# Moving layer-norm statistics of a Mamba and mixture-of-experts layer from GpSimd to ScalarE and VectorE

## The chip, the cores and the metric

The kernel runs on one core of a Trainium2 chip. The metric is device time in microseconds (us), the median of several runs of the whole kernel. A core has five engines with a queue of their own each: TensorE (PE in the profile, its weight loads PEld), VectorE (DVE), ScalarE (ACT), GpSimd (POOL) and SyncE (SP, which issues DMAs). Each engine runs its own instructions in the order in which they were written, and engines wait for one another through semaphores.

## The reference

One layer of a sequence model over x of 32 sequences, 512 tokens, 256 features, all in float32. Cut to what matters here:

```python
def _layernorm(x, axis=-1, eps=1e-05):
    m = jnp.mean(x, axis=axis, keepdims=True)
    v = jnp.var(x, axis=axis, keepdims=True)
    return (x - m) / jnp.sqrt(v + eps)

def _L0_attn_ref(x, ln_g, ln_b, ...):
    skip = x
    xn = (x - mu) * jax.lax.rsqrt(var + 1e-05) * ln_g + ln_b
    xp, z = split(xn @ in_proj_w.T)                  # 512 channels each
    xc = silu(causal depthwise conv of 4 taps (xp) + conv_b)
    dt, Bm, Cm = split(xc @ x_proj_w.T)              # 16, 16, 16
    dt = softplus(dt @ dt_proj_w.T + dt_proj_b)
    A = -jnp.exp(A_log)
    # h_t = exp(dt_t * A) * h_{t-1} + dt_t * xc_t * Bm_t ; y_t = sum_n h_t * Cm_t
    y = _selective_scan(xc, dt, A, Bm, Cm, D) * silu(z)
    g = gelu(y @ out_proj_w.T) @ glu_w.T + glu_b
    return g[..., :256] * sigmoid(g[..., 256:]) + skip

def _L0_ffn_ref(x, ...):
    shared = (silu(gu[:, :512]) * gu[:, 512:] @ shared_down_w) * sigmoid(x @ shared_gate_w)
    probs = softmax(x @ gate_w)                      # 64 experts, the best 8 of each token
    # each expert takes its first 128 tokens: silu(gate) * up, then down, weighted
    return y + shared

x = x + _L0_attn_ref(_layernorm(x), ...)
x = x + _L0_ffn_ref(_layernorm(x), ...)
```

So the first block normalizes twice in a row (once outside, once inside with its own eps). From the variance v of x one needs (v + eps)^(-1/2) and, for the two norms as one, (v (1 + eps) + eps^2)^(-1/2).

## The kernel before

The 32 sequences run one after the other. A sequence of 512 tokens takes 32 steps s: two halves of the 512 channels times 16 states n. A step works on one tile of 128 partitions x 1024 (two channel blocks of 512 tokens). In each step:

- ACT writes the two decays exp(dt * A) into PSUM (`decays`, L537), two steps ahead;
- POOL multiplies dt*x by B into a ring of eight tiles (`scan_input`, L377), three steps ahead;
- DVE runs the scan along the tokens (L1165) and multiplies the state by C (L1175); for the 15 steps of the table `ON_POOL`, POOL makes that product instead (`read_state`, L386);
- PE adds the transposed product to a sum in PSUM (`sum_states`, L814).

The first product of half 0 (`y` times silu(z)) is taken by DVE at step 18, that of half 1 at step 2 of the next sequence (`gate_y`, L1078), once PE has summed all 16 states.

Around this skeleton every engine carries, inside the same 32 steps, the work that comes after the scan of the sequence before ("post": out projection, gelu, gated unit, second norm, router, shared expert) and the work ahead of the scan of the next one ("prep": norm, input projection, conv, silu, dt). What is done at which step is written by hand in a table of numbers at the end of the file (`SOFT_AT`, `SCALES2`, `NORM2` and so on); each engine walks through it in order of s, and within a step in the order of its own function `turn`. The first two and last two sequences are written out, the 28 between are a hardware loop of 14 rounds with two sequences each, so every second change of sequence is also the loop's jump. Behind the 32 sequences stands the stage of the 64 experts (gathers, small matmuls, scatters).

The places that matter here:

- `moments` (L1051, L1055): mean and variance of x by DVE, for the first norm at step 20 (`MOMENTS0`, two sequences ahead), for the second at step 15 (`MOMENTS2`).
- `scales_x` (L390 to L407, POOL, step 29) forms from them the two reciprocal roots with `pow`, the shifts -mean * root, and 1 + root, six small instructions; `scales_x1` (L409 to L419, POOL, step 15) the same for the second norm, four instructions.
- ACT uses them in `norm_x` (L545, step 1), `sum_x` (L552, step 17) and `norm_x1` (L560, step 15).
- `step_sizes` (L428) and `step_inputs` (L433, L435) on POOL: a DMA that adds two parts of dt in memory, then dt times x, then a mark at the first token. The mark (`dt_ready`) releases the decays of the next sequence on ACT and its scan inputs on POOL. For half 0 they stand at steps 28 and 29, for half 1 at 8 and 9. In POOL's queue `scales_x` stands ahead of `step_inputs` of step 29.
- softplus on ACT: `soft_exp` (L614) and `soft_log` (L619), the logarithm at steps 27 and 6.
- After silu_z (L597, step 29) ACT's next work is the decays of the next sequence; at step 0 `read_dt` (L608, L609) copies the two last dt blocks of half 1, between which PE has to run `project_dt` (L858) and after which PE sums the last state (L814).

ACT holds one set of function tables at a time; the program loads a set (ACT_TABLE_LOAD) ahead of an activation whose function is not in the one that is held.

Of the kernel before, what the change touches and what calls it, by code (L numbers as in the profile page):

```python
# [9 lines left out]
ALU = mybir.AluOpType  # L10
# [30 lines left out]
def mamba_moe(nc, x, vectors, in_wT, conv_w, x_wT, dt_wT, a_log, out_wT, glu_wT, router_w, sgu_w, sdown_w, egu_w, edown_w, out, counts, table, ends, bc):  # L41
    ctx = ExitStack()
    with ctx:
# [43 lines left out]
        minus_half = sb("minus_half", [P, 2 * NT])  # L87
# [58 lines left out]
        scales0_ready, scales2_ready = sem("scales0_ready"), sem("scales2_ready")  # L146
        prep_full, prep_read = sem("prep_full"), sem("prep_read")
# [204 lines left out]
        def _(pool):  # L352
# [4 lines left out]
            pool.memset(minus_half[:, :], -0.5).then_inc(cleared, 1)  # L357
# [32 lines left out]
            def scales_x(k):  # L390
                wait_apart(pool, ln0, 3 * k + 2)
                pool.tensor_scalar(rstd[:, 0, :].unsqueeze(2), mv[:, 0, :, 1:2], EPS, None, ALU.add)\
                    .then_inc(scales0_ready, 1)
                pool.tensor_scalar(rstd[:, 1, :].unsqueeze(2), mv[:, 0, :, 1:2], 1.0 + EPS, EPS * EPS,
                                   ALU.mult, ALU.add).then_inc(scales0_ready, 1)
                pool.tensor_scalar(keep[:, :].unsqueeze(2), mv[:, 0, :, 0:1], -1.0, None, ALU.mult)\
                    .then_inc(scales0_ready, 1)
                pool.wait_ge(scales0_ready, 6 * k + 2)
                pool.tensor_tensor(rstd[:, 0:2, :], rstd[:, 0:2, :],  # L399
                                   minus_half[:, :].rearrange("p (a i) -> p a i", a=2), ALU.pow)\  # L400
                    .then_inc(scales0_ready, 1)
# [35 lines left out]
            def turn(b, h, prep, post):  # L437
                p, q = b + 1, b - 1
                for s in range(NS):
# [4 lines left out]
                    if post and s == SCALES2:  # L444
                        scales_x1(q)
# [75 lines left out]
        def _(act):  # L521
# [199 lines left out]
            def post_at(q, h, s):  # L721
# [11 lines left out]
                if s == G_AT[1] + AFTER_G:  # L733
                    glu_gate(q)
# [636 lines left out]
```

## Time and profile before

| | us |
|---|---|
| median of 3 runs | 4621.09 |
| lowest and highest | 4621.03, 4624.51 |
| profiled execution, from its first to its last instruction (span) | 4617.3 |
| median less that span (start and end of the run around it) | 3.8 |
| first scan starts at about | 96 |
| last of the 32 sequences ends its scans at about | 4178 |
| mean granted TensorE clock, share of full speed | 0.886 |

The profile's page lists busy time per engine over the span. The 32 sequences take most of it, one after the other in about 128 us each; the last tenth is the stage of the experts. An engine's busy share tells how full it is, not whether others wait for it; that is read from the waits and from the order of time around one change of sequence.

### The profile page before, as it was taken

The numbers are of one execution on the slowest core, as the hardware profiler recorded it, in microseconds if no ns is written. First come the engines' busy times: TensorE is split into PE (matmuls) and PEld (weight loads), VectorE is DVE, ScalarE is ACT, GpSimd is POOL, SyncE is SP. The second block draws the span as 40 slices with busy tenths as digits, with TensorE's granted clock in tenths as the row PEclk, the third lists the DMA queues.
The fourth block names the chain that finished last, engine by engine and source line by source line (L and its number), as shares of the span: only waits on it lengthen the run. The fifth ranks groups of instructions, "written<-read, shape, count | busy, mean of one in ns | idle before, by whom it ended". The sixth has DMA issues, their size and how long they took to land.

```text
span 4617.3 us, 56113 instructions
## 1 busy us (share of the span) xinstructions
PE 3632.1 (79%) x16000; PEld 2285.9 (50%) x16000; DVE 3829.4 (83%) x3990; ACT 3280.2 (71%) x4895; POOL 4074.0 (88%) x2223
## 2 busy tenths in 40 slices
PE   3588888888888888888888888888888888876465
PEld 1354555555545555555555545554555454553344
DVE  2899989898989988889989999888989899882433
ACT  3687778787777877878777777787877778772111
POOL 3999999999999999999999999999999999991576
PEclk7798999899999989999989999999989999988666
DMA  3222222222222222222222222222222221220665
GB/s 121 87 75 74 79 80 99 95 99 99 94 100 75 72 66 94 96 98 100 99 95 99 75 72 72 88 99 95 99 99 94 100 75 71 74 77 17 173 158 131
DMA packets 147381, 423.30 MB, mean 92 GB/s; under 512 B 15520, under 2 KB 98656, under 8 KB 113776
## 3 DMA queue, kind: packets, MB, share of 16 engines
q1 hardware_dynamic: 123504, 362.73, 21.3%
q0 software_dynamic: 23552, 56.64, 6.5%
q8 instruction: 154, 2.52, 0.2%
q14 instruction: 171, 1.40, 0.1%
HBM read 333.17 MB, written 52.59 MB: 84 GB/s over the span
## 4 chain that ended last, share of the span: by engine, by line
POOL 39%; issue 22%; DVE 19%; PE 9%; ACT 8%; DMA 2%; POOLq 0%; DVEq 0%; ACTq 0%; SPq 0%
POOL hs L377 19%; POOL hs L386 13%; DVE ps L1165 9%; ACT ps L537 3%; DVE hs L1165 3%; PE ps L884 2%; DVE hs L1175 2%; PE ps L814 2%; DVE xc L1069 2%; POOL dtu L433 2%; PE ps L858 1%; POOL hs L473 1%; POOL rstd L399 1%; DVE xn L1090 1%; ACT L537 1%
## 5 line engine op out<-in xcount | busy, mean ns | idle before, releaser
L377 POOL TENSOR_TENSOR hs<-dtu,b_all 128x1024 f32<-128x1024 f32 x1024 | 2409.4, 2373 | 3.4
L537 ACT ACTIVATE ps<-dt,neg_a 128x512 f32<-128x512 f32 x2048 | 1327.2, 682 | 290.0 <-DVE hs L1175 146.5
L814 PEld LDWEIGHTS ps<-ident,hs 128*128 128x128 f32 x8192 | 1013.9, 151 | 584.9 <-issue 393.3
L1165 DVE TENSOR_TENSOR_SCAN ps<-ps,hs 128x1024 f32<-128x1024 f32 x544 | 1244.2, 2287 | 46.0 <-ACT ps L537 23.8
L814 PE MATMUL ps<-ident,hs 128*128 128x128 f32 x8192 | 1151.4, 290 | 117.3 <-POOL hs L386 75.8
L1165 DVE TENSOR_TENSOR_SCAN hs<-ps,hs 128x1024 f32<-128x1024 f32 x480 | 1088.1, 2278 | 170.2 <-ACT ps L537 147.4
L386 POOL TENSOR_TENSOR hs<-hs,c_all 128x1024 f32<-128x1024 f32 x480 | 1137.0, 2369 | 59.5 <-DVE hs L1165 46.1
L1175 DVE TENSOR_TENSOR hs<-ps,c_all 128x1024 f32<-128x1024 f32 x544 | 665.7, 1224 | 34.4
L924 PE MATMUL ps<-mT,w_sgu 128*128 128x512 f32 x1024 | 522.4, 635 | 12.5 <-DVE hid L1122 9.0
L858 PE MATMUL ps<-xd,w_dt 32*128 32x512 f32 x256 | 185.3, 810 | 234.0 <-ACT dt L609 223.1
L537 ACT ACT_TABLE_LOAD x219 | 281.0, 1283 | 117.3 <-POOL dt L435 113.9
L884 PE MATMUL ps<-mT,w_glu 128*128 128x512 f32 x512 | 275.7, 666 | 99.3 <-ACT hid L637 77.0
L1069 DVE SCALAR_TENSOR_TENSOR xc<-ps,cw_sb,xc 128x509 f32<-128x509 f32 (+2 forms) x384 | 285.9, 745 | 48.7 <-ACT xc L575 39.7
L838 PE MATMUL ps<-xnT,w_in 128*128 128x512 f32 x512 | 257.9, 627 | 56.6 <-DVE xc L1069 54.2
L845 PE MATMUL ps<-w_in,xnT 128*128 128x512 f32 x512 | 277.0, 669 | 9.5 <-ACT sz L582 4.8
L924 PEld LDWEIGHTS ps<-mT,w_sgu 128*128 128x128 f32 x1024 | 185.9, 203 | 172.0 <-issue 134.6
L875 PE MATMUL ps<-hid,w_out 128*128 128x512 f32 x512 | 238.0, 608 | 38.6 <-ACT hid L623 37.9
L932 PE MATMUL ps<-w_sd,hid 128*128 128x256 f32 x1024 | 237.2, 385 | 24.9 <-DVE hid L1122 22.8
L932 PEld LDWEIGHTS ps<-w_sd,hid 128*128 128x128 f32 x1024 | 189.5, 190 | 60.8 <-DVE hid L1122 30.8
L433 POOL TENSOR_TENSOR dtu<-dt,xc 128x1024 f32<-128x1024 f32 x64 | 151.3, 2364 | 57.6 <-DMA dt<-dtu 57.6
L858 PEld LDWEIGHTS ps<-xd,w_dt 32*128 32x128 f32 x256 | 44.6, 217 | 308.9 <-ACT dt L609 281.8
L582 ACT COPY sz<-ps 128x512 f32<-128x512 f32 x128 | 73.9, 577 | 168.5 <-PE ps L845 168.5
(127 smaller groups left out, 4448.9 us busy)
## 6 DMA issues: line engine op xcount, KB each, us to landing
b_all<-bc SPq DMA_DIRECT2D x128, 1024.0 KB, 6.0
c_all<-bc SPq DMA_DIRECT2D x128, 1024.0 KB, 7.9
dt<-dtu POOLq DMA_DIRECT2D x64, 512.0 KB, 4.6
table<-rows SPq DMA_DIRECT2D x32, 640.0 KB, 3.8
xin<-x SPq DMA_DIRECT2D x32, 512.0 KB, 3.5
out<-mT SPq DMA_DIRECT2D x32, 512.0 KB, 3.7
c_all<-egu_w SPq DMA_DIRECT2D x64, 256.0 KB, 2.8
c_all<-edown_w SPq DMA_DIRECT2D x64, 128.0 KB, 3.0
```

What stands on the lines that cost most here:

```text
L377: pool.tensor_tensor(ring(h, hf, n), dtu[:, JH * hf:JH * hf + JH, :], b_all[:, n, :].unsqueeze(1).broadcast_to([P, JH, L]), ALU.mult)\
L386: pool.tensor_tensor(ring(h, hf, n), ring(h, hf, n), c_all[:, n, :].unsqueeze(1).broadcast_to([P, JH, L]), ALU.mult)\
L537: i = act.activation(state_of(n)[:, k, :], dt[:, j, :], ACT.Exp, scale=neg_a[:, j, n:n + 1])
L814: m = pe.matmul(ybank[:, i, k * P:(k + 1) * P], ring(h, hf, n)[:, k, i * P:(i + 1) * P], ident[:, :], start=False, stop=(n == N - 1), is_t ...
L845: m = pe.matmul(prbank, xnT[:, f, i * P:(i + 1) * P], w_in[:, f, DI:2 * DI], start=(f == 0), stop=(f == FM - 1))
L858: pe.matmul(prbank, w_dt[:, j * P:(j + 1) * P], xd[0:2 * R, :], start=True, stop=True)\
L884: m = pe.matmul(pobank, w_glu[:, k, col:col + P], mT[:, k, :], start=(k == 0), stop=(k == FM - 1))
L924: m = pe.matmul(pobank, w_sgu[:, f, block * P:(block + 1) * P], x2T[:, f, :], start=(f == 0), stop=(f == FM - 1))
L932: m = pe.matmul(po_tok[:, i, :], hid[:, k, (2 * c + i) * P:(2 * c + i + 1) * P], w_sd[:, k, :], start=(k == 0), stop=(k == KS - 1))
L1069: dve.scalar_tensor_tensor(xc[:, j, back:L], prbank[:, 0:L - back], cw_sb[:, j, k:k + 1], xc[:, j, back:L], ALU.mult, ALU.add)\
L1165: dve.tensor_tensor_scan(inputs if s in ON_POOL else whole, whole, inputs, 0.0, ALU.mult, ALU.add).then_inc(state_ready, 1)
L1175: dve.tensor_tensor(ring(h, hf, n), state_of(n), c_all[:, n, :].unsqueeze(1).broadcast_to([P, JH, L]), ALU.mult)\
```

## The change

The reciprocal roots move from POOL to ACT, as exp(-0.5 * ln(v * scale + eps)), with eps from a small tile in place of the tile of -0.5. The shifts become one instruction each on DVE. POOL keeps no statistics. A set that holds both the exponential and the logarithm is loaded by name at the start and right behind every activation whose function is in another set (silu, gelu, sigmoid), so the logarithm of softplus no longer loads one. In the table of steps the first norm's roots move to step 22 and its shift to step 24; the second norm's use, and the router's steps behind it, move one step later. The core of the diff (left out: the semaphores' declarations and the removed POOL code of `scales_x` and `scales_x1`, described above):

```diff
@@ scalar engine @@
+            def exponents():
+                act.preload_act_table_set("natural_log_exp_and_others")
+
+            exponents()
...
+            def scales_x(p):
+                act.wait_ge(ln0, 3 * p + 2)
+                act.activation(rstd[:, 0, :].unsqueeze(2), mv[:, 0, :, 1:2], ACT.Ln, bias=eps[:, 0:1])
+                act.activation(rstd[:, 1, :].unsqueeze(2), mv[:, 0, :, 1:2], ACT.Ln, bias=eps[:, 1:2],
+                               scale=1.0 + EPS).then_inc(scales0_ready, 1)
+                act.wait_ge(scales0_ready, 3 * p + 1)
+                act.activation(rstd[:, 0:2, :], rstd[:, 0:2, :], ACT.Exp, scale=-0.5).then_inc(scales0_ready, 1)
+                act.wait_ge(scales0_ready, 3 * p + 2)
+                act.activation(keep[:, :], rstd[:, 0, :], ACT.Identity, bias=1.0).then_inc(scales0_ready, 1)
+
+            def scales_x1(q):
+                act.wait_ge(ln2, 3 * q + 2)
+                act.activation(rstd[:, 2, :].unsqueeze(2), mv[:, 1, :, 1:2], ACT.Ln, bias=eps[:, 0:1])\
+                    .then_inc(scales2_ready, 1)
+                act.wait_ge(scales2_ready, 2 * q + 1)
+                act.activation(rstd[:, 2, :], rstd[:, 2, :], ACT.Exp, scale=-0.5).then_inc(scales2_ready, 1)
+
             def norm_x(p):
-                act.wait_ge(scales0_ready, 6 * p + 6)
+                act.wait_ge(shift0_ready, p + 1)
...
             def silu_x(p):
                 act.wait_ge(prep_read, p * PREP_USES + PREP_X[J - 1] + 1)
                 act.activation(xc[:, :, :], xc[:, :, :], ACT.Silu).then_inc(xc_ready, 1)
+                exponents()
...
@@ the same call behind silu_z, gelu, glu_gate and hid_silu; in ACT's post_at and turn: @@
+                if s == SCALES2:
+                    scales_x1(q)
                 if s == NORM2:
                     norm_x1(q)
...
+                    if s == SCALES0 and not (isinstance(b, int) and b + 2 >= B):
+                        scales_x(b + 2)
...
@@ vector engine @@
+            def shift_x(p):
+                dve.wait_ge(scales0_ready, 3 * p + 2)
+                wait(dve, xs_ready, p)
+                dve.scalar_tensor_tensor(shift[:, 0:2, :],
+                                         mv[:, 0, :, 0:1].rearrange("p i o -> p o i").broadcast_to([P, 2, NT]), -1.0,
+                                         rstd[:, 0:2, :], ALU.mult, ALU.mult).then_inc(shift0_ready, 1)
+
+            def shift_x1(q):
+                dve.wait_ge(scales2_ready, 2 * q + 2)
+                dve.scalar_tensor_tensor(shift[:, 2, :].unsqueeze(2), mv[:, 1, :, 0:1], -1.0,
+                                         rstd[:, 2, :].unsqueeze(2), ALU.mult, ALU.mult).then_inc(shift2_ready, 1)
...
@@ table of steps @@
-SCALES0 = 29
+SCALES0 = 22
+SHIFT0 = 24
 SCALES2 = 15
-NORM2 = 15
+SHIFT2 = 16
+NORM2 = 16
-XT_AT = (16, 16)
-R_AT = 17
-ROUTER_EXP = 18
-SG_AT = (18, 19, 20, 22)
+XT_AT = (17, 17)
+R_AT = 18
+ROUTER_EXP = 19
+SG_AT = (19, 20, 21, 22)
```

GpSimd's queue at the end of a sequence (steps 28 and 29), before. Here L428 is the DMA that adds to dt, L377 a scan input, L386 a product with C, L433 and L435 dt times x and the mark:

```order
L428 DMA dt<-dtu 128x1024 [waits soft]
L377 TENSOR_TENSOR hs<-dtu,b_all 128x1024 [waits summed]
L386 TENSOR_TENSOR hs<-hs,c_all 128x1024 [waits state_ready]
L392 TENSOR_SCALAR rstd<-mv 128x4 [waits ln0]
L394 TENSOR_SCALAR rstd<-mv 128x4
L396 TENSOR_SCALAR keep<-mv 128x4
L399 TENSOR_TENSOR rstd<-rstd,minus_half 128x8 [waits scales0_ready]
L403 TENSOR_TENSOR shift<-rstd,keep 128x8 [waits scales0_ready]
L407 TENSOR_SCALAR keep<-rstd 128x4 [waits scales0_ready]
L433 TENSOR_TENSOR dtu<-dt,xc 128x1024 [waits dt_added0]
L435 MEMSET dt 128x2 [waits dt_ready]
L377 TENSOR_TENSOR hs<-dtu,b_all 128x1024 [waits summed,b_in0,dt_ready]
```

The same place in the changed kernel, where L398, L379, L388, L403 and L405 are the lines that were L428, L377, L386, L433 and L435:

```order
L398 DMA dt<-dtu 128x1024 [waits soft]
L379 TENSOR_TENSOR hs<-dtu,b_all 128x1024 [waits summed]
L388 TENSOR_TENSOR hs<-hs,c_all 128x1024 [waits state_ready]
L403 TENSOR_TENSOR dtu<-dt,xc 128x1024 [waits dt_added0]
L405 MEMSET dt 128x2 [waits dt_ready]
L379 TENSOR_TENSOR hs<-dtu,b_all 128x1024 [waits summed,b_in0,dt_ready]
```

Between the product with C and dt times x, six instructions are gone; nothing else moved there.

ScalarE's queue from the logarithm of softplus (step 27) to the decays of the next sequence, before. L537 are decays, L619 the logarithm, L658 and L661 the router's weights, L597 silu of z, L592 a scaling of the conv's output:

```order
L537 ACTIVATE ps<-dt,neg_a 128x512 x2
L619 ACT_TABLE_LOAD
L619 ACTIVATE dtu<-dtu 128x1024
L537 ACT_TABLE_LOAD
L537 ACTIVATE ps<-dt,neg_a 128x512 x4
L658 ACTIVATE maskb<-rep 128x256
L661 ACTIVATE rows<-pr,small 128x64 x4
L597 ACT_TABLE_LOAD
L597 ACTIVATE sz<-sz 128x2048
L537 ACT_TABLE_LOAD
L537 ACTIVATE ps<-dt,neg_a 128x512 x2
L592 ACTIVATE xc<-xc,vecs 128x512 x2
```

The same place in the changed kernel (L504 decays, L605 logarithm, L646 and L649 weights, L582 silu of z, L486 the load by name, L577 the scaling):

```order
L504 ACTIVATE ps<-dt,neg_a 128x512 x2
L605 ACTIVATE dtu<-dtu 128x1024
L504 ACTIVATE ps<-dt,neg_a 128x512 x4
L646 ACTIVATE maskb<-rep 128x256
L649 ACTIVATE rows<-pr,small 128x64 x4
L582 ACT_TABLE_LOAD
L582 ACTIVATE sz<-sz 128x2048
L486 ACT_TABLE_LOAD
L504 ACTIVATE ps<-dt,neg_a 128x512 x2
L577 ACTIVATE xc<-xc,vecs 128x512 x2
```

The two loads around the logarithm are gone. The load behind silu of z is now an instruction of its own; in the queue before, it is part of the decays behind it and shares their wait for `dt_ready`. Over one sequence 14 loads become 10.

ScalarE's queue at steps 21 to 24, before. L586 is silu of the conv's output, L675 copies of the shared expert's gate, L602 the copy of dt, B and C, L679 silu of the shared expert, L608 and L609 `read_dt`:

```order
L675 COPY hid<-ps 128x512
L586 ACT_TABLE_LOAD
L586 ACTIVATE xc<-xc 128x2048
L537 ACT_TABLE_LOAD
L537 ACTIVATE ps<-dt,neg_a 128x512 x4
L675 COPY hid<-ps 128x512
L602 COPY xd<-ps 64x512
L537 ACTIVATE ps<-dt,neg_a 128x512 x2
L679 ACT_TABLE_LOAD
L679 ACTIVATE hid<-hid 128x2048
L608 ACTIVATE dtu<-ps,vecs 128x512
L609 ACTIVATE dt<-ps,vecs 128x512
```

The same place in the changed kernel, from behind silu of the conv's output (L663 the gate's copies, L509 to L515 the statistics, L588 the copy of dt, B and C, L667 silu of the shared expert, L594 `read_dt`):

```order
L486 ACT_TABLE_LOAD
L504 ACTIVATE ps<-dt,neg_a 128x512 x2
L663 COPY hid<-ps 128x512
L509 ACTIVATE rstd<-mv,eps 128x4
L510 ACTIVATE rstd<-mv,eps 128x4
L513 ACTIVATE rstd<-rstd 128x8
L515 ACTIVATE keep<-rstd 128x4
L504 ACTIVATE ps<-dt,neg_a 128x512 x2
L663 COPY hid<-ps 128x512
L667 ACT_TABLE_LOAD
L667 ACTIVATE hid<-hid 128x2048
L594 ACTIVATE dtu<-ps,vecs 128x512
```

Four small activations and one copy of the gate now stand between the decays of two steps, and a load stands ahead of `read_dt` instead of behind it.

## Rows read from the trace of the kernel before

**Rows 1.** Profile page, busy time by engine and the chain that ended last, whole span.

```profile
PE 3632.1 (79%) x16000; PEld 2285.9 (50%) x16000; DVE 3829.4 (83%) x3990; ACT 3280.2 (71%) x4895; POOL 4074.0 (88%) x2223
POOL 39%; issue 22%; DVE 19%; PE 9%; ACT 8%; DMA 2%; POOLq 0%; DVEq 0%; ACTq 0%; SPq 0%
```

**Rows 2.** Waits, whole span: who <- whom, us in total, times, longest.

```profile
DVE hs L1165 <- ACT ps L537: 147.4, 64, 35.1
...
DVE ps L1165 <- POOL hs L377: 21.9, 36, 2.3
...
DVE hs L1165 <- POOL hs L377: 15.5, 5, 8.4
```

**Rows 3.** DVE in order of time, two changes of sequence: start, us, line, [idle before <-releaser].

```profile
2014.20 2.29 DVE L1165 TENSOR_TENSOR_SCAN hs<-ps,hs 128x1024 f32<-128x1024 f32 x1 [2.10 <-ACT ps L537]
...
2023.98 1.23 DVE L1078 TENSOR_TENSOR sz<-ps,sz 128x1024 f32<-128x1024 f32 x1 [1.50 <-PE ps L814]
...
2142.43 2.29 DVE L1165 TENSOR_TENSOR_SCAN hs<-ps,hs 128x1024 f32<-128x1024 f32 x1 [3.25 <-ACT ps L537]
...
2154.42 1.23 DVE L1078 TENSOR_TENSOR sz<-ps,sz 128x1024 f32<-128x1024 f32 x1 [2.91 <-PE ps L814]
```

**Rows 4.** POOL in order of time, ahead of the first of these changes.

```profile
2000.13 0.80 POOL L428 DMA_DIRECT2D dt<-dtu  x1
...
2005.73 0.23 POOL L392 TENSOR_SCALAR rstd<-mv 128x4 f32<-128x4 f32 x1
...
2008.85 2.36 POOL L433 TENSOR_TENSOR dtu<-dt,xc 128x1024 f32<-128x1024 f32 x1
```

**Rows 5.** ACT in order of time, the same two changes.

```profile
2006.06 1.91 ACT L597 ACTIVATE sz<-sz 128x2048 f32<-128x2048 f32 x1
2011.57 1.28 ACT L537 ACT_TABLE_LOAD   x1 [3.60 <-POOL dt L435]
...
2017.43 1.30 ACT L537 ACTIVATE ps<-dt,neg_a 128x512 f32<-128x512 f32 x2
...
2140.72 1.30 ACT L537 ACTIVATE ps<-dt,neg_a 128x512 f32<-128x512 f32 x2
...
2147.88 1.30 ACT L537 ACTIVATE ps<-dt,neg_a 128x512 f32<-128x512 f32 x2 [2.50 <-DVE ps L1165]
```

**Rows 6.** PE in order of time, the first of these changes.

```profile
2014.15 1.12 PE L858 MATMUL ps<-xd,w_dt 32*128 32x512 f32 x2
2019.97 2.07 PE L858 MATMUL ps<-xd,w_dt 32*128 32x512 f32 x2 [4.69 <-ACT dt L609]
```

**Rows 7.** Busy us (instructions) of PE, PEld, DVE, ACT, POOL; granted PEclk; DMA share, GB/s.

```profile
2019.90:2022.00 2.10, 2.03 (x3) 0.53 (x3) 2.10 (x2) 0.01 (x1) 2.10 (x2) 0.50 1.04 355
```

**Rows 8.** Profile page, DMA issues: count, KB each, median us from issue to landing.

```profile
dt<-dtu POOLq DMA_DIRECT2D x64, 512.0 KB, 4.6
```

**Rows 9.** Groups by line, DVE, whole span: count, busy us, mean ns, idle before.

```profile
L1203 DVE SCALAR_TENSOR_TENSOR dt<-dt,row_of 128x16 f32<-128x16 f32 x4 | 0.8, 198 | 0.0
```

**Rows 10.** ACT and DVE in order of time, inside one sequence (steps 14 to 28).

```profile
2077.87 1.31 ACT L537 ACTIVATE ps<-dt,neg_a 128x512 f32<-128x512 f32 x2
...
2090.34 0.20 ACT L652 ACTIVATE small<-lg 128x4 f32<-128x4 f32 x1
2090.57 0.20 ACT L654 ACTIVATE small<-small 128x4 f32<-128x4 f32 x1
...
2110.05 0.58 ACT L675 COPY hid<-ps 128x512 f32<-128x512 f32 x1
...
2118.00 1.30 ACT L537 ACTIVATE ps<-dt,neg_a 128x512 f32<-128x512 f32 x2
...
2079.39 2.27 DVE L1165 TENSOR_TENSOR_SCAN ps<-ps,hs 128x1024 f32<-128x1024 f32 x1
...
2091.12 2.30 DVE L1165 TENSOR_TENSOR_SCAN ps<-ps,hs 128x1024 f32<-128x1024 f32 x1 [0.55 <-POOL hs L377]
...
2122.26 0.69 DVE L1122 TENSOR_TENSOR hid<-ps,hid 128x512 f32<-128x512 f32 x1 [0.64 <-PE ps L924]
```

More of the change, by code:

```diff
@@ L356, in _ @@
             pool.memset(w_dt[:, :], 0.0).then_inc(cleared, 1)
-            pool.memset(minus_half[:, :], -0.5).then_inc(cleared, 1)
+            pool.memset(eps[:, 0:1], EPS).then_inc(cleared, 1)
+            pool.memset(eps[:, 1:2], EPS * EPS).then_inc(cleared, 1)
             pool.wait_ge(cleared, CLEARED)
@@ L437, in turn @@
             def turn(b, h, prep, post):
-                p, q = b + 1, b - 1
+                p = b + 1
                 for s in range(NS):
@@ L443, in turn @@
                         step_inputs(b, 1)
-                    if post and s == SCALES2:
-                        scales_x1(q)
-                    if s == SCALES0 and not (isinstance(b, int) and b + 2 >= B):
-                        scales_x(b + 2)
                     if prep and s == SIZES[0]:
@@ L642, in glu_gate @@
                 act.activation(sg, sg, ACT.Sigmoid).then_inc(gate_done, 1)
+                exponents()
             def read_x2T(q, f):
@@ L767, in _ @@
                 decays(0, 0, 0, n)
+            scales_x(1)
             turns(act, turn)
@@ L1059, in moments_x @@
                 dve.wait_ge(x_loaded, 16 * p + 16)
-                wait(dve, scales0_ready, 6 * p)
+                wait(dve, scales0_ready, 3 * p)
                 moments(ln0, 0, p, xin)
+            def shift_x(p):
[8 more added lines that the diff above has]
+                                         rstd[:, 2, :].unsqueeze(2), ALU.mult, ALU.mult).then_inc(shift2_ready, 1)
             def conv(p, j):
@@ L1140, in post_at @@
                     moments_x1(q)
+                if s == SHIFT2:
+                    shift_x1(q)
                 if s == R_AT + AFTER_R:
@@ L1183, in turn @@
                         moments_x(b + 2)
+                    if s == SHIFT0 and not (isinstance(b, int) and b + 2 >= B):
+                        shift_x(b + 2)
             moments_x(0)
+            shift_x(0)
             for s in range(NS):
@@ L1188, in _ @@
             moments_x(1)
+            shift_x(1)
             turns(dve, turn)
@@ L1269 @@
 LOADS, POST_LOADS = 7, 5
-CLEARED = 5
+CLEARED = 6
 LAG = 2
```

42 lines of the change are left out of this document (7 added, 35 removed).

## The prediction, made before the changed kernel ran

> **What bounds the kernel now.** I read the page first, then the waits, then the order of time of the engines around two neighbouring changes of sequence, in that order because the page alone misleads. The page shows POOL as the fullest engine and as 39% of the chain that ended last [rows 1], which looks as if every microsecond taken from POOL came off the end. The waits say otherwise: over the whole run DVE stands still for a scan input of POOL 21.9 us in 36 short waits and 15.5 us in five more, one of them 8.4 us, but for the decays of ACT 147.4 us, 35.1 of it once at the start [rows 2]. POOL is full, and yet DVE seldom waits for it.
>
> The order of time shows where DVE does wait. One sequence takes 128.2 us (first scan at 2014.20, then at 2142.43) [rows 3]. Call E the moment at which DVE has nothing left of the old sequence: it is the scan's start less its idle time, 2012.10 and 2139.18 [rows 3]. The product L1078 with which DVE closes the old sequence begins 11.9 us after E in the first change and 15.2 us after E in the second, which is the loop's jump as well; the mean is 13.6 us. DVE has work for some 8.1 us of that (three scans of 2.29 and one product of 1.23, as long as these rows); the rest is waiting, for ACT first and for PE at the end [rows 3].
>
> What makes ACT late: POOL issues the DMA on dt at 2000.13, comes to the six statistics at 2005.73, starts dt times x at 2008.85 [rows 4] and sets the mark behind it. ACT ended silu of z at 2007.97, then stood for 3.60 us until the mark, then loaded its table from 2011.57 to 2012.85, and only then wrote decays [rows 5]. From there it works without a gap: decays, scaling, decays, the counts, the decays of step 2 at 2017.43 [rows 5], `read_dt`. PE waits for that until 2019.97, runs its product in 2.07 us where the one before took 1.12 [rows 6], with the granted clock at 0.50 in that stretch, the lower level of 1.2 GHz [rows 7], then sums the last state until DVE may start at 2023.98. So the place to look at is this chain: POOL's statistics, the mark, ACT's load, ACT's work, PE, L1078. It is walked 31 times.
>
> **The change, part by part.**
>
> *POOL at the change of sequence.* The six instructions between 2005.73 and 2008.85 go, 3.12 us [rows 4]. Is dt there by then? The DMA issued at 2000.13 lands 4.6 us later in the median [rows 8], at 2004.7, so dt times x can start at 2005.73, and the mark comes at about 2008.3 in place of 2011.5. The late one is now ACT: silu of z ends at 2007.97 [rows 5], and the load, which no longer waits for the mark, ends 1.28 us later, at 2009.25. Decays start there and not at 2012.85: 3.6 us earlier.
>
> *The first scan.* The decays take 1.30 us [rows 5], end at 2010.55, before E, so in the plain change the scan follows E at once (2.10 us gained). In the other change the decays ended at 2142.02 [rows 5], but the scan began at 2142.43 [rows 3]: something of DVE's own held it, and I take that to be the loop's jump. There I count no gain, and the scan stays 3.25 us behind E.
>
> *The closing product.* ACT's row of work up to the end of `read_dt` has one link that cannot move with it: the decays of step 2 need the scan of step 0. Plain change: scan ends at E+2.3, decays 1.3, `read_dt` 1.2 us, so E+4.8; PE then needs 4.0 us as now (2019.97 to 2023.98) or 2.2 us if it keeps the faster clock of its 1.12 us product. That is E+8.8 or E+7.0, and DVE's own work ends at E+8.1. So L1078 starts at E+8.1 to 8.8 instead of 11.9: 3.1 to 3.8 us. With the jump: scan ends at E+5.55, `read_dt` at E+8.05 (ACT's own jump, 2.50 us [rows 5], fits ahead of that), L1078 at E+12.1 or, bound by DVE, E+11.3, instead of 15.2: 3.1 to 3.9 us. PE stands idle 4.69 us before that product now [rows 6] and about 1.6 us then, so part of the slow clock should go; I take **3.5 us** of a range of 3.1 to 3.9.
>
> *New work on DVE.* Two instructions of 8 and 4 elements. The nearest row, the same operation with two operands in SBUF on 16 elements, took 0.198 us [rows 9]: 0.2 each. The second one also waits: ACT's decays of step 17 end at 2079.18, then come logarithm and exponential at 0.23 us a piece, as two dependent small activations follow each other now [rows 10], so 2079.65, and DVE is free at 2079.39 [rows 10]: about 0.3 us. Sum 0.7 us later. The bound below is 0.4 (no wait). Above: no row of the loop shows a DVE instruction with two SBUF tensors beside POOL's products, and the row of 0.198 is from the expert stage, where POOL makes none. At worst such an instruction waits out a POOL product of 2.36 us [rows 4], 4.7 us for two. The Trainium skill, GPSIMD Engine Reference, section Key points, speaks for that end: it names contention between GpSimd and VectorE instructions with two SBUF inputs, without a figure. I take 0.2, since the measured operation is the same and 8 elements leave little to contend for, and price the other end as a rival.
>
> *POOL inside the sequence.* POOL also loses the four statistics of step 15. The wait of 0.55 us at step 20 [rows 10] is the only one on POOL that DVE has in this sequence; it goes: 0.5 us gained. The rest of POOL's freed time costs and gives nothing, since DVE isn't waiting for it.
>
> *New work on ACT at steps 21 to 24.* Four small activations, 0.23 us each, 0.9 us, and a copy of the gate (0.58 us [rows 10]) that now stands between the same decays; what little idle time ACT has there takes a part of these 1.5 us, so I take it that the decays of step 27 come 1.2 us later. They end at 2119.30 now [rows 10] and their scan starts at 2119.33 (2122.26 less 0.64 less 2.29 [rows 10]): no slack. DVE will be 0.2 us later itself (0.7 less 0.5), so it stalls about 1.0 us; but the 0.64 us for which it waits for PE right behind that scan [rows 10] is absorbed. Net 0.4 us lost, between 0 and 1.3.
>
> *Table loads.* Four of 14 per sequence go, 4 x 1.28 x 32 = 164 us of ACT's time. I cost that at nothing: ACT's idle time covers it, as in each of those places it next waits for a DVE readout. The load in the chain is already counted. The moved use of the second norm (one step later, router behind it) I cost at nothing too: DVE reads the router's output one step later with no wait of its own, and PE's shared-expert steps end at the same step 22. Without that cover the price is the 0.64 us of the PE wait above.
>
> *Start and end.* The roots of sequence 1 now stand behind ACT's first decays, and DVE's first scan behind them: about 2 us later, once; the last sequence's second norm loses some 1 us of POOL work. I take 1 us of loss.
>
> *Sum.* Per change 3.5 - 0.7 + 0.5 - 0.4 = 2.9 us; 31 changes give 90 us, less 1. The profiled span of 4617.3 becomes 4528, and with the 3.8 us around it, which put the median of the runs at 4621.09, the time is **4532 us**, 1.9% faster. With every term at its good end (3.9 - 0.4 + 0.5 + 0.2 for waits at PE that go with an earlier POOL = 4.2) it is 4491, with ACT's and DVE's terms at the bad end but no contention (3.1 - 0.7 + 0.5 - 1.3 = 1.6) 4572.
>
> **Rivals.**
>
> *POOL bounds after all.* The chain of 39% speaks for it [rows 1], the few waits of DVE for POOL against it [rows 2]. Then the freed POOL time would come off whole: 3.12 us and, for four instructions instead of six, at most as much again, 6.2 us per change, 193 us: 4428. Chance 0.08.
>
> *Slower: the shift waits out GpSimd.* Each of DVE's two shifts holds until POOL's running product has ended, at worst 2.36 us [rows 4], so 4.7 us a sequence instead of 0.4. Then 2.9 - 4.3 = -1.4 us, 31 times: 4665. It decides from 1.65 us for each shift on (0.2 and half of 2.9). For it: POOL runs products almost without a gap. Against it: such small operands. That rule of the Trainium skill (GPSIMD Engine Reference, Key points) points this way; the trace of before neither shows nor excludes it. Chance 0.08, with other ways to end slower.
>
> *ACT gives it back.* If the later decays of steps 25 to 28 don't cost 0.4 but stall DVE 2.5 us (1.3 at step 27, and 1.2 more at step 28 because `read_dt` now stands behind a table load), the gain is 0.8 us per change: 4597. For it: ACT has no idle time from step 23 to 28. Against: at step 28 DVE is already late. Chance 0.12.
>
> *Only another wait takes the place.* dt's DMA lands late, or the jump sits on both changes, and the closing product waits for PE as long as now: within 0.2%. The DMA's 4.6 us and the plain change speak against it. Chance 0.05.
>
> **How the numbers follow.** The forecast keeps 0.67. About 0.2% (9 us) is what a measurement of this kernel can tell from no change. Faster: 0.67 + 0.08 + 0.12 = 0.87; same 0.05; slower 0.08. The range reaches over the forecast's bounds, 4491 to 4572, to the case in which ACT gives it back, and a little below for waits that I don't see: 4470 to 4600. It leaves out the POOL-bound case, the slower one and most of no change.
>
> **What would show it.** Right: the time from one first scan to the next near 125 us; the scan of step 0 close behind E in the plain change and unmoved in the jump; ACT's table load directly behind silu of z with no wait; L1078 some 8 to 9 and 11 to 12 us behind E; the second PE product below 2 us; DVE's shifts at 0.2 us; ten table loads per sequence. Wrong: shifts of 1 us and more or long idle time ahead of the scan that follows them; DVE idle for ACT at steps 25 to 28 by more than 1 us; ACT still waiting for POOL's mark; a sequence of 122 us or less, which would mean that POOL was the bound.

## The result and the profile after

The changed kernel took 4999.24 us (median of 4 runs, 4963.95 to 5011.92) beside 4621.06 us of the kernel before: ratio 1.0814, 95% interval 1.0792 to 1.0836. It is 8% slower; forecast was 4532 us, with 4470 to 4600 as the range. The profiled execution took 5011.92 us, its span 5010.2.

The page, busy time and chain, against [rows 1]:

```profile
PE 3748.1 (75%) x16000; PEld 2392.3 (48%) x16000; DVE 4064.3 (81%) x4054; ACT 3171.7 (63%) x4963; POOL 3938.0 (79%) x1904
issue 26%; DVE 22%; POOL 20%; PE 19%; ACT 10%; DMA 2%; DVEq 0%; POOLq 0%; ACTq 0%; SPq 0%
```

POOL and ACT have less to do, as intended. But DVE, which got 64 instructions of 8 and 4 elements, is busy 235 us longer. The groups of DVE by line show where (busy us, mean ns | idle before), against [rows 9]:

```profile
L1067 DVE SCALAR_TENSOR_TENSOR shift<-mv,rstd 128x4 f32<-128x4 f32 x32 | 199.3, 6228 | 9.3 <-ACT rstd L522 9.0
L1061 DVE SCALAR_TENSOR_TENSOR shift<-mv,rstd 128x8 f32<-128x8 f32 x32 | 46.3, 1448 | 33.9 <-ACT rstd L513 33.9
```

The two shifts take 7.7 us a sequence, where 0.4 was forecast. The waits over the whole run (who <- whom: us in total, times, longest), against [rows 2]:

```profile
POOL hs L388 <- DVE hs L1174: 634.1, 157, 10.2
ACT xd L588 <- PE ps L848: 129.8, 31, 5.2
PE ps L919 <- ACT hid L663: 117.4, 52, 3.5
```

POOL now waits for DVE's scans, 634.1 us in all. The other two say that ACT's copy of dt, B and C (L588) waits for PE's projection of x (L848), and PE's shared-expert product (L919) for ACT's gate copy (L663). The same three in the kernel before:

```profile
POOL hs L386 <- DVE hs L1165: 46.1, 38, 2.5
ACT xd L602 <- PE ps L853: 6.0, 1, 6.0
PE ps L924 <- ACT hid L675: 2.7, 4, 0.7
```

**At these two changes the turn did what was forecast.** DVE in order of time at two changes of sequence, against [rows 3] (L1085 is the closing product that was L1078):

```profile
2047.38 2.29 DVE L1174 TENSOR_TENSOR_SCAN hs<-ps,hs 128x1024 f32<-128x1024 f32 x1 [3.11 <-POOL hs L379]
...
2056.51 1.22 DVE L1085 TENSOR_TENSOR sz<-ps,sz 128x1024 f32<-128x1024 f32 x1 [0.75 <-PE ps L809]
...
2183.87 2.28 DVE L1174 TENSOR_TENSOR_SCAN hs<-ps,hs 128x1024 f32<-128x1024 f32 x1
...
2191.78 1.21 DVE L1085 TENSOR_TENSOR sz<-ps,sz 128x1024 f32<-128x1024 f32 x1
```

In the plain change (2183.87) the scan follows with no idle time, and the closing product starts at E + 7.9 us (forecast 8.1 to 8.8, before 11.9). In the change with the jump the scan stays 3.11 us behind E, and the product starts at 2056.51 - (2047.38 - 3.11), E + 12.2 us (forecast 11.3 to 12.1, before 15.2). The gain is 4.0 and 3.0 us, the mean 3.5. The links show too: ACT's load stands behind silu of z with no wait where it had stood 3.60 us [rows 5]; in the plain change PE waits 1.68 us, not 4.69, for the second product, which takes 1.12, not 2.07 [rows 6], with the granted clock at 1.00, the level of 2.4 GHz, not 0.50 [rows 7]. ACT, PE, and the engines' busy time in that stretch:

```profile
2177.92 1.91 ACT L582 ACTIVATE sz<-sz 128x2048 f32<-128x2048 f32 x1
2179.85 1.28 ACT L486 ACT_TABLE_LOAD   x1
```

```profile
2188.82 1.12 PE L853 MATMUL ps<-xd,w_dt 32*128 32x512 f32 x2 [1.68 <-ACT dt L595]
```

```profile
2188.80:2190.00 1.20, 1.19 (x3) 0.43 (x4) 1.20 (x2) 0.03 (x1) 1.20 (x1) 1.00 1.08 337
```

**Where it was lost.** The mean time from one scan's start to the next, over sequences 3 to 27, gives a map by step (worked out from the scans' starts in each trace; the best variant stands beside it, the experiments lead to it):

| steps | before | after | best (x11) |
|---|---|---|---|
| 31, 0, 1, 2 (the turn) | 20.8 | 17.4 | 17.8 |
| 16 (the second shift) | 2.3 | 9.1 | 2.2 |
| 17 to 20 | 19.3 | 20.8 | 19.3 |
| 23, 24 (the first shift) | 5.6 | 7.3 | 5.8 |
| 25, 26, 27 | 12.0 | 18.6 | 12.7 |
| a whole sequence | 128.3 | 141.8 | 126.6 |

Steps 16 and 24 are the shifts. One short and one long occurrence of the second shift, DVE and then POOL in order of time:

```profile
2111.31 1.67 DVE L1067 SCALAR_TENSOR_TENSOR shift<-mv,rstd 128x4 f32<-128x4 f32 x1 [0.16 <-ACT rstd L522]
...
2247.72 11.35 DVE L1067 SCALAR_TENSOR_TENSOR shift<-mv,rstd 128x4 f32<-128x4 f32 x1 [0.28 <-ACT rstd L522]
2258.99 2.29 DVE L1174 TENSOR_TENSOR_SCAN ps<-ps,hs 128x1024 f32<-128x1024 f32 x1
```

```profile
2110.58 2.38 POOL L388 TENSOR_TENSOR hs<-hs,c_all 128x1024 f32<-128x1024 f32 x1
...
2247.51 2.35 POOL L379 TENSOR_TENSOR hs<-dtu,b_all 128x1024 f32<-128x1024 f32 x1
2249.82 2.33 POOL L388 TENSOR_TENSOR hs<-hs,c_all 128x1024 f32<-128x1024 f32 x1
2252.13 6.92 POOL L379 TENSOR_TENSOR hs<-dtu,b_all 128x1024 f32<-128x1024 f32 x3
```

The short one ends at 2112.98 with POOL's running product (2112.96). The long one begins with a product and ends with the fifth (2259.07 and 2259.05), when POOL has nothing left: its next product needs a scan that stands behind the shift in DVE's queue and starts 10.2 us after the shift's end, the longest of POOL's waits for DVE. Such waits are a part of POOL's 634.1 us; without shifts on DVE (x3 below) 422.3 us are still there. Of the 32 second shifts 14 took 11.3 to 13.3 us and ended when POOL had run out of work; 17 ended with the product that was running when they began, and the last one took 0.16 us, with no product beside it.

Steps 25 to 27 are another matter. ACT from silu of the conv's output on, and PE, in order of time:

```profile
2285.80 1.92 ACT L570 ACTIVATE xc<-xc 128x2048 f32<-128x2048 f32 x1
2287.73 1.28 ACT L486 ACT_TABLE_LOAD   x1
2289.02 1.30 ACT L504 ACTIVATE ps<-dt,neg_a 128x512 f32<-128x512 f32 x2
2290.26 0.57 ACT L663 COPY hid<-ps 128x512 f32<-128x512 f32 x1
...
2297.44 0.58 ACT L588 COPY xd<-ps 64x512 f32<-64x512 f32 x1 [3.94 <-PE ps L848]
...
2302.46 1.28 ACT L486 ACT_TABLE_LOAD   x1
2303.75 0.69 ACT L594 ACTIVATE dtu<-ps,vecs 128x512 f32<-128x512 f32 x1
```

```profile
2290.89 1.98 PE L919 MATMUL ps<-mT,w_sgu 128*128 128x512 f32 x4 [3.50 <-ACT hid L663]
2293.68 3.65 PE L848 MATMUL ps<-xc,w_x 128*64 128x512 f32 x8
2298.28 1.12 PE L853 MATMUL ps<-xd,w_dt 32*128 32x512 f32 x2
2300.26 1.88 PE L919 MATMUL ps<-mT,w_sgu 128*128 128x512 f32 x4
2305.07 1.12 PE L853 MATMUL ps<-xd,w_dt 32*128 32x512 f32 x2 [2.93 <-ACT dt L595]
```

The same silu on ACT, and on PE the projection of x and the second product with dt, in the kernel before:

```profile
2104.09 1.92 ACT L586 ACTIVATE xc<-xc 128x2048 f32<-128x2048 f32 x1
```

```profile
2106.14 3.64 PE L853 MATMUL ps<-xc,w_x 128*64 128x512 f32 x8
...
2116.74 1.33 PE L858 MATMUL ps<-xd,w_dt 32*128 32x512 f32 x2 [1.72 <-ACT dt L609]
```

The change moved the third copy of the shared expert's gate from step 20 to 21, which in ACT's queue is from ahead of silu to behind it, its reload and one pair of decays. PE's next gate product waits 3.50 us for that copy, and the projection of x (L848), which stands behind it in PE's queue, starts at 2293.68, 6.0 us after the end of silu at 2287.72; before, it was 0.1 us (2106.01 to 2106.14). ACT then waits 3.94 us for the projection, and its decays come late. Behind silu of the shared expert the load at 2302.46 now stands ahead of `read_dt`, and PE waits 2.93 us for that, where it had waited 1.72. The occurrence shown is a mild one: its gate product took 1.98 us at a granted clock of 1.00, but in 20 of the 30 waits of this kind the clock was lower. In x3 below, the same product behind the same wait took 3.66 us, with a granted clock of 0.51 from 2181.30 to 2184.70, close to 0.50, the level of 1.2 GHz:

```profile
2181.25 3.66 PE L929 MATMUL ps<-mT,w_sgu 128*128 128x512 f32 x4 [3.50 <-ACT hid L673]
```

### The profile page after: what moved, and what is told of

It is laid out like the page before. It is cut to its first block, busy times and chain, and to the rows that moved or that the text cites. A ratio compares the mean times of both kernels' runs of the same rounds, so it can differ in the third digit from the quotient of the medians.

```text
span 5010.2 us, 55761 instructions
## 1 busy us (share of the span) xinstructions
PE 3748.1 (75%) x16000; PEld 2392.3 (48%) x16000; DVE 4064.3 (81%) x4054; ACT 3171.7 (63%) x4963; POOL 3938.0 (79%) x1904
## 4 chain that ended last, share of the span: by engine, by line
issue 26%; DVE 22%; POOL 20%; PE 19%; ACT 10%; DMA 2%; DVEq 0%; POOLq 0%; ACTq 0%; SPq 0%
POOL hs L379 12%; DVE ps L1174 10%; DVE hs L1174 4%; POOL hs L388 4%; PE ps L927 4%; ACT ps L504 3%; PE ps L809 3%; PE ps L919 3%; DVE xc L1076 2%; ACT L486 2%; PE ps L848 2%; PE ps L879 1%; DVE hs L1184 1%; PE ps L798 1%; PE ps L853 1%
## 5 line engine op out<-in xcount | busy, mean ns | idle before, releaser
L379 POOL TENSOR_TENSOR hs<-dtu,b_all 128x1024 f32<-128x1024 f32 x1024 | 2414.4, 2379 | 6.4 <-PE ps L809 1.5
L388 POOL TENSOR_TENSOR hs<-hs,c_all 128x1024 f32<-128x1024 f32 x480 | 1140.3, 2376 | 643.1 <-DVE hs L1174 634.1
L504 ACT ACTIVATE ps<-dt,neg_a 128x512 f32<-128x512 f32 x2048 | 1325.6, 682 | 473.8 <-DVE hs L1184 267.0
L809 PEld LDWEIGHTS ps<-ident,hs 128*128 128x128 f32 x8192 | 1060.1, 154 | 526.6 <-issue 452.2
L809 PE MATMUL ps<-ident,hs 128*128 128x128 f32 x8192 | 1183.4, 296 | 70.4 <-issue 39.5
L919 PE MATMUL ps<-mT,w_sgu 128*128 128x512 f32 x1024 | 559.9, 674 | 122.3 <-ACT hid L663 117.4
L919 PEld LDWEIGHTS ps<-mT,w_sgu 128*128 128x128 f32 x1024 | 198.0, 215 | 298.9 <-issue 147.6
L853 PE MATMUL ps<-xd,w_dt 32*128 32x512 f32 x256 | 168.7, 742 | 172.4 <-ACT dt L595 171.4
L896 PE MATMUL ps<-ident,rows 128*128 128x128 f32 x256 | 62.1, 388 | 253.7 <-ACT rows L544 184.0
L1067 DVE SCALAR_TENSOR_TENSOR shift<-mv,rstd 128x4 f32<-128x4 f32 x32 | 199.3, 6228 | 9.3 <-ACT rstd L522 9.0
L403 POOL TENSOR_TENSOR dtu<-dt,xc 128x1024 f32<-128x1024 f32 x64 | 158.8, 2481 | 58.7 <-DMA dt<-dtu 58.7
```

Of the source, the lines that this page charges most:

```text
L379: pool.tensor_tensor(ring(h, hf, n), dtu[:, JH * hf:JH * hf + JH, :], b_all[:, n, :].unsqueeze(1).broadcast_to([P, JH, L]), ALU.mult)\
L388: pool.tensor_tensor(ring(h, hf, n), ring(h, hf, n), c_all[:, n, :].unsqueeze(1).broadcast_to([P, JH, L]), ALU.mult)\
L504: i = act.activation(state_of(n)[:, k, :], dt[:, j, :], ACT.Exp, scale=neg_a[:, j, n:n + 1])
L809: m = pe.matmul(ybank[:, i, k * P:(k + 1) * P], ring(h, hf, n)[:, k, i * P:(i + 1) * P], ident[:, :], start=False, stop=(n == N - 1), is_t ...
L919: m = pe.matmul(pobank, w_sgu[:, f, block * P:(block + 1) * P], x2T[:, f, :], start=(f == 0), stop=(f == FM - 1))
```

## The experiments

The theory after this reading: three separate costs, the shifts beside POOL's products, the moved gate copy, and the load ahead of `read_dt`. The rivals: that the shifts are slow for another reason than POOL, that the moved router steps cost and not the gate, or that ACT's statistics and loads cost as such.

**An operation with two SBUF tensors, alone.** To the kernel before, one instruction is added in DVE's queue whose result nobody reads; x1 has it at step 16, x5 at step 24 (the declaration of `extra` and its filling are left out).

```diff
+                if s == 16:
+                    dve.scalar_tensor_tensor(extra[:, 2, :], extra[:, 0, :], -1.0, extra[:, 1, :], ALU.mult, ALU.mult)
```

> The kernel before, plus one VectorE instruction per sequence at step 16 that multiplies two small SBUF tiles of 4 elements (same operation as the new shift); nobody waits for its result. Theory C (a VectorE instruction with two tensors in SBUF gets in only when GpSimd ends a product, sometimes several products later): the instruction shows 1.5 to 12 us, 4 to 6 us in the mean, and the time grows by 2 to 6 us a sequence: 4680 to 4800 us. Theory D (the shift is long because its data come late or the operation itself is slow): 0.2 us each, 4621 to 4630 us.

> The same extra instruction with two SBUF tensors in the kernel before, now at step 24, where GpSimd runs products without a gap (at step 16 it stood among GpSimd's small statistics). Nobody waits for its result. Theory C: it lasts until GpSimd ends a product, 0.7 to 2.3 us or several products, and the time grows by 0.5 to 6 us a sequence: 4635 to 4800 us. Theory D (a VectorE instruction like this is short wherever it stands): 0.2 to 0.3 us, 4619 to 4625 us.

x1: 4620.50 us, ratio 1.0004 (0.9994 to 1.0013). x5: 4818.04 us, ratio 1.0424 (1.0404 to 1.0444). The groups by line of x1 and then of x5:

```profile
L1145 DVE SCALAR_TENSOR_TENSOR extra<-extra 128x4 f32<-128x4 f32 x32 | 10.4, 326 | 0.0
```

```profile
L1145 DVE SCALAR_TENSOR_TENSOR extra<-extra 128x4 f32<-128x4 f32 x32 | 246.3, 7698 | 0.0
```

x1 came out where the theory of a short instruction puts it, but by itself it decided nothing: at its place POOL is just ending a small instruction, and the operation slips in there (0.14 us in most sequences). The same instruction between POOL's products takes 7.7 us and costs 200 us in all, a little over the expected range, with nothing else changed. So it is the company that makes the shift slow, not the operation.

**The shift with one SBUF tensor.** In the changed kernel each shift becomes four `tensor_scalar` whose mean is a scalar operand (the lines taken out and the second norm's loop, the same with one element, are left out):

```diff
+                for i in range(NT):
+                    m = dve.tensor_scalar(shift[:, 0:2, i], rstd[:, 0:2, i], mv[:, 0, i, 0:1], -1.0, ALU.mult, ALU.mult)
```

> The changed kernel with the shift as four VectorE instructions for each norm that read one tensor from SBUF and the mean as a scalar for each partition. Theory C: these take 0.1 to 0.2 us each, the waits of 6.2 and 1.4 us go, and the time falls below that of before, 4530 to 4600 us. Theory D (late data, or any VectorE instruction at this place is held): still over 4900 us. In between, 4620 to 4750 us, if the longer ScalarE work at steps 21 to 28 costs by itself.

4867.70 us, ratio 1.0541 (1.0523 to 1.0558), in none of the three expected ranges. Groups by line:

```profile
L1062 DVE TENSOR_SCALAR shift<-rstd,mv 128x2 f32<-128x2 f32 x128 | 194.7, 1585 | 33.7 <-ACT rstd L513 33.7
L1068 DVE TENSOR_SCALAR shift<-rstd,mv 128x1 f32<-128x1 f32 x128 | 18.4, 206 | 12.0 <-ACT rstd L522 11.5
```

Half a cure: the form with one element per partition is free of it (step 16 falls from 9.1 to 3.1 us), the form with two is not (step 24 rises from 3.4 to 8.4).

**No shift on DVE at all.** ACT forms the shifts, by `activation` with the negated mean as its scale, behind the roots.

> The changed kernel with the shifts made by ScalarE too (one negation and four small activations for each norm), none by VectorE. Theory C: VectorE's long instructions are gone; ScalarE has 2 x 5 more small activations of 0.2 to 0.3 us, so the second norm comes 1.2 us later and the decays of steps 25 to 28 another 1.2 us: 4560 to 4680 us. Theory D: no fall below 4900 us unless VectorE itself was the slow one.

4792.05 us, ratio 1.0372 (1.0355 to 1.0389). Against the changed kernel 207 us are back, 6.7 a sequence; step 16 is at 2.25 us. That is less than either theory said: the shifts on DVE were one cost, but the kernel is still slower than before, by steps 25 to 27 above all (19.1 us).

**The moved steps.** x7 is the kernel before with the steps of the second norm, router and gate alone moved as in the change; x6 is x3 with only the gate's steps back.

```diff
 (x6)
-SG_AT = (19, 20, 21, 22)
+SG_AT = (18, 19, 20, 22)
```

> The kernel before, statistics on GpSimd and loads as before, with only the second norm's use and the router's and gate's steps moved as in the change. Theory R: 2.2 us at step 19, where VectorE waits for logits that PE makes behind the first state products, and 2 to 4 us at steps 25 to 27: 4740 to 4810 us. If the steps are hidden, as the prediction had it: 4610 to 4630 us.

> The changed kernel with the shifts on ScalarE (4792 us) and the shared expert's gate steps put back from 19, 20, 21, 22 to 18, 19, 20, 22. Theory R (the third gate's copy now stands behind silu of the conv's output in ScalarE's queue, PE waits for it 3.5 us at the lower clock, dt's product and the decays of steps 26 and 27 are late): 2.5 to 4.5 us a sequence come back, 4655 to 4715 us. Theory A (the four small statistics and the shifts on ScalarE themselves make the decays late): 4770 to 4795 us.

x7: 4856.79 us, ratio 1.0520 (1.0502 to 1.0537), with no statistic moved; that is 238 us or 7.7 a sequence, above the expected range. x6: 4651.64 us, ratio 1.0074 (1.0057 to 1.0091), 140 us less than x3 by one edit, the copy's step. The waits of x7 and of x6 (L924 and L929 are the gate product, L675 and L673 the copy):

```profile
ACT xd L602 <- PE ps L853: 133.3, 31, 5.6
PE ps L924 <- ACT hid L675: 119.4, 49, 3.5
```

```profile
ACT xd L598 <- PE ps L858: 4.2, 1, 4.2
PE ps L929 <- ACT hid L673: 2.9, 5, 0.7
```

Both waits come with the moved steps and go with the gate's. Steps 25 and 26 together fall from 13.9 us in x3 to 9.2 (before 8.4); step 27 stays late, at 5.3 (before 3.5), and steps 17 to 20 at 21.2 (before 19.3).

**The load ahead of `read_dt`.** x4 is the kernel before with the loads by name alone; x9 is x6 with the load behind silu of the shared expert moved behind the first block that `read_dt` copies.

```diff
 (x9, in hid_silu and in read_dt's step)
-                exponents()
...
+                        if j == 0:
+                            exponents()
```

> The kernel before with the set of exponential and logarithm loaded by name behind silu, gelu and sigmoid, statistics still on GpSimd. If the chain at the change of sequence (mark, table load, decays) sets the time, the load of 1.28 us leaves it: 1.0 to 1.5 us a sequence, 4575 to 4590 us. If ScalarE's loads are hidden everywhere: 4615 to 4625 us.

> x6_gate_steps_back with one edit: behind hid silu the Ln/Exp table set is loaded only after the first read of the time step's block, so that read no longer stands behind a load. Theory L (a load ahead of read_dt makes TensorE wait for it, and the sequence's steps 26 and 27 end later): step 27 falls from 5.29 towards the 3.53 us of the kernel before and the sequence loses 1.5 to 2.4 us, over 31 sequences 47 to 75 us: 4577 to 4605 us against 4651.6 of x6. Rival (the wait at step 27 only shows time that is late from the steps ahead): the load's 1.3 us comes back elsewhere, 4640 to 4660 us.

x4: 4627.04 us, ratio 1.0017 (1.0008 to 1.0027), in neither expected range; its ten runs spread from 4613.81 to 4633.56, and the trace is that of the lowest. In it the turn alone gains 2.0 us a sequence (31, 0, 1, 2: 18.8 us), and step 27 gives 1.9 back (3.5 to 5.4). x9: 4584.77 us, ratio 0.9917 (0.9901 to 0.9934), 67 us less than x6 (74 if each is taken against the kernel before that ran beside it); step 27 falls from 5.3 to 2.8 us. The waits of DVE's product on the shared expert, in x6 and in x9:

```profile
DVE hid L1127 <- PE ps L929: 84.3, 36, 3.9
```

```profile
DVE hid L1128 <- PE ps L930: 11.9, 7, 3.8
```

**The router, and the place of ACT's statistics.** x10 is x9 with second norm and router back at their steps; x11 is x10 with the roots at step 20, ahead of silu, instead of 22.

```diff
 (x10)                    (x11)
-NORM2 = 16               -SCALES0 = 22
+NORM2 = 15               +SCALES0 = 20
-XT_AT = (17, 17)
+XT_AT = (16, 16)
-R_AT = 18
+R_AT = 17
-ROUTER_EXP = 19
+ROUTER_EXP = 18
```

> x9 with the remaining moved steps put back where the kernel before had them (second norm 15, transposes 16, router 17, its exponentials 18); statistics and shifts stay on ScalarE, the tables are loaded by name. None of the three suspected costs (an addition on VectorE beside GpSimd's products, moved steps, a load ahead of read_dt) is left. Theory of three costs: the turn's gain of about 3 us a sequence is left over and some of it goes to ScalarE's statistics: 4535 to 4580 us, faster than before. Rival (ScalarE's statistics and shifts cost as much as the turn gives): 4600 us or more.

> x10 with the statistics of the next sequence's first norm issued at step 20, ahead of silu, where ScalarE has idle time, instead of behind it. If ScalarE's statistics are what x10 still pays in steps 21 to 24: 0.5 to 1.4 us a sequence less than x10, 15 to 43 us. If they are covered already: within 10 us of x10.

x10: 4574.37 us, ratio 0.9901 (0.9879 to 0.9923); 10 us less than x9, with intervals that overlap, so the place of the second norm and the router costs nothing that these runs can tell here. x11: 4548.95 us, ratio 0.9835 (0.9818 to 0.9851), 25 us less than x10 and 1.65% faster than before. The wait of DVE for the decays, in x10 and in x11, shows from where; the last fence is x11's busy time by engine:

```profile
DVE hs L1171 <- ACT ps L505: 109.9, 95, 30.8
```

```profile
DVE hs L1171 <- ACT ps L505: 73.5, 53, 31.1
```

```profile
PE 3636.1 (80%) x16000; PEld 2304.9 (51%) x16000; DVE 3823.1 (84%) x3990; ACT 3210.9 (71%) x5283; POOL 3934.0 (86%) x1904
```

x11 is the best of all: roots and shifts on ACT, GpSimd without statistics, and none of the three costs. What it moves ahead of silu is nine small activations, for ACT makes the shifts here too; in the changed kernel there were four.

**The other way: POOL keeps the statistics.** x8 is the kernel before with the loads by name (that behind silu of the shared expert late) and `scales_x`, roots and shifts as before, at step 31, behind the mark in POOL's queue; x12 has it at step 0 of the next sequence. Of x8's edit, without the loads:

```diff
-SCALES0 = 29
+SCALES0 = 31
```

> The kernel before with GpSimd's six statistics moved from step 29 to step 31, behind the mark of dt, and the loads by name, the one behind silu of the shared expert only after the first dt block is read. The prediction's term for the change of sequence (mark 3.1 us and load 1.3 us earlier): 2.5 to 3.7 us a sequence, 4505 to 4545 us. If the wait only moves to GpSimd's third scan input, which now stands behind the statistics: 4570 to 4620 us.

> x8_statistics_last (kernel before, tables loaded by name, GpSimd's statistics and VectorE's shift behind the mark at step 31) with GpSimd's statistics issued at step 0 of the next sequence, ahead of input 3. If x8 still pays for GpSimd's statistics at the turn (scan 2 waits 0.45 us for GpSimd there): about 1 us a sequence less, 4545 to 4565 us against 4576.9. If they only move from one wait into another: 4570 to 4590 us.

x8: 4576.91 us, ratio 0.9915 (0.9898 to 0.9931), in the range of the wait that only moves. x12: 4569.11 us, ratio 0.9884 (0.9868 to 0.9901), just below its range of the same kind. The turn's steps tell what it was: they take 18.8 us in x8 and 18.8 in x4, where POOL's statistics stand ahead of the mark as before. So some two thirds of the turn's gain (2.0 us of 3.0 in x11) come from the loads by name alone, without moving any arithmetic, and putting POOL's statistics behind the mark added nothing at the turn: step 31 falls from 6.8 us in x4 to 6.4, and step 1 rises from 3.5 to 4.3. What x8 has over x4, 50 us, is step 27 with the late load (5.4 to 3.8). Nor did the further microsecond come that x12 was to bring: 8 us in all, 0.25 a sequence, because the turn's steps only went from 18.8 to 18.6 us. Waits for POOL move there from one scan to the next: DVE waits 35.1 and 14.6 us for scan inputs in x8 (scans into PSUM and into SBUF), 23.1 and 28.5 us in x12.

## Why the prediction was wrong

The sum failed at three terms: the price of a shift on DVE (0.2 us, measured 6.2 and 1.4), the moved steps of the gate and the place of a table load (both at nothing, measured 4.5 and 2.2 us a sequence). By medians, with one edit at a time from the changed kernel (the kernel before was at 4618 to 4625 us beside them):

| step | us | change | us a sequence (of 31) |
|---|---|---|---|
| the change | 4999.2 | | |
| shifts off DVE (x3) | 4792.1 | -207.2 | 6.7 |
| gate copy back (x6) | 4651.6 | -140.4 | 4.5 |
| load behind `read_dt`'s first block (x9) | 4584.8 | -66.9 | 2.2 |
| router back (x10) | 4574.4 | -10.4 | not told from 0 |
| roots ahead of silu (x11) | 4549.0 | -25.4 | 0.8 |

1. *The closing product, +3.5 us*: about right. In the changed kernel it is 4.0 and 3.0 us in the two changes shown and 3.4 over the turn's steps, link by link, the clock of PE's product included. But the turn also shortens when DVE is late for another reason: in x5, where nothing of the change is there, the hold at step 24 alone brings the turn's steps from 20.8 to 17.8 us. So a part of the 3.4 may be luck; in x11, without those delays, the turn's steps gain 3.0, a little under the forecast's 3.1 to 3.9. And the shares are other than the text has them: it put POOL's six statistics, 3.12 us, at the head of the chain, but the loads by name alone give 2.0 of the 3.0 (x4), which leaves 1.0 for POOL without its statistics.

2. *The shifts, -0.7 us*: the step that failed most. The price of 0.2 us was that of an operation with POOL idle, and it was taken because "8 elements leave little to contend for". It measured 6.2 and 1.4 us; that the operands were small did not help, and the smaller of the two shifts took the longer, for the instruction waits and does not work. The rival "the shift waits out GpSimd" named the mechanism and the place, but had a chance of 0.08 and a worst price of one product, 2.36 us; it can be five in a row. The Trainium skill (GPSIMD Engine Reference, Key points) names contention of GpSimd with VectorE instructions that have two SBUF inputs. The traces agree that it is there: 0.14 us behind a small POOL instruction (x1), 7.7 us among POOL's products (x5).

3. *The moved steps, costed at nothing*: wrong for the gate. For the router it held where x10 tests it. The text looked at the router's output and at the last gate step, 22, and passed over the third copy, whose move by one step crosses silu, a reload and decays in ACT's queue. The price given for a lost cover, 0.64 us, was that of a wait on DVE; the runs show 4.5 us a sequence, since PE's projection of x stands behind the gate product. In the kernel before the same moves cost 7.7 us a sequence (x7: steps 25 to 27 18.0 instead of 12.0 us, steps 17 to 20 20.9 instead of 19.3), more than gate and router cost in the changed kernel's variants; that difference is open.

4. *ACT at steps 21 to 24, -0.4 us, loads at nothing*: the rival "ACT gives it back" had it. It put 1.3 us on the statistics and 1.2 on the load ahead of `read_dt`, 2.5 together; x11 and x9 measured 0.8 and 2.2, 3.0 together, though the 0.8 are with the shifts on ACT too, and the load's cost stood at step 27, where the text had it at step 28. In the forecast the load was counted as four loads saved, and the place of one that stays was not looked at, although the two queues stand side by side in the section on the change.

5. *POOL bounds after all*: refuted. Without statistics POOL is busy 3934.0 us in x11, 140 less than before, and the kernel gained some 75 us, where 193 were expected if POOL bounds.

6. *The small terms.* POOL inside the sequence, +0.5 us: DVE's waits for POOL ahead of scans into PSUM did go (21.9 us before, 4.6 in x11), but steps 17 to 20 take 19.3 us in both, for what step 19 gains (0.6 us) steps 17 and 18 lose. Start and end, 1 us of loss: wrong in sign. The first scan starts at 92.0 us in the changed kernel and 90.9 in x11, not after 96.4, and behind the last scan there are 436.5 and 434.2 us instead of 438.8.

Without its three costs, and with the roots ahead of silu, the change is worth 72 to 76 us (4621 to 4549, or 1.65%) where the sum said 89. That is nearer than the mechanism: of the 67.5 us between the two profiled spans 57 lie between the first scan and the last, 1.9 us a change where the sum had 2.9; the other 10 come at start and end, which the text had as a loss. Still open is what decides whether a shift waits for one product or until POOL runs out of work: both kinds begin at much the same points of a running product.

## What to carry to other kernels

Price a small instruction by what its engine neighbours do at that moment, never by the same operation elsewhere; where a profile has no row for the pair, add the instruction at that very place to the kernel before and time it, as x5 does, and choose a place at which the neighbour works (x1 did not). When a table of steps moves by one, go through each engine's queue and look at what each entry crosses, and for a load that becomes an instruction of its own, at what now stands behind it. A gain at one place can be forecast about right and drown in three places that were costed at little or nothing. And a wait that got shorter in the changed kernel proves little while that kernel is late elsewhere; x5 shortens the turn without touching it.

## What the hardware showed that was not expected

- One and the same DVE instruction with two SBUF tensors, 4 elements wide, took between 161 and 13,249 ns; beside GpSimd's products it ended with the running one in 17 of 31 cases and, in the other 14, only when GpSimd had none left. The Trainium skill (SBUF — State Buffer, section "SBUF: two separate sides") has the shared port pair as an exclusive lock that whoever starts first holds for the whole instruction. The trace agrees that DVE is shut out, and differs in how long: by that rule, with products of 2.4 us, one product would be the most, and five passed.
- Such a hold costs both engines: the scan behind the shift stands too, and POOL, out of work, waits for it. With the shifts off DVE (x3) POOL's wait for the scans falls from 634.1 to 422.3 us, and x5's one instruction brings it from 46.1 us to 189.0.
- `tensor_scalar` with one element per partition took 206 ns beside the same products, with two elements 1585 ns. The Trainium skill (VectorE: DVE Perf Modes, section "What auto-detection actually checks") lets the engine take a mode that uses both read ports (2×_2P) when a single source and the destination lie in SBUF and their outermost dimensions other than 1 are both even or equal; two elements have such a dimension, one has none. The two times agree with that, but no run here shows the mode itself.
